# A hybrid attention kernel: batch 0's neighbourhood scores straight from fp32 projections, the others from stacks made behind it

## The chip, the cores and the metric

The kernel runs on one core of one Trainium2 chip. Its time is the device time in microseconds (us) of one execution; the median over the runs counts. The engines are TensorE (PE in the profile; PEld is its weight load, which overlaps its matmuls), VectorE (DVE), ScalarE (ACT), GpSimd (POOL) and SyncE (SP, which here only issues DMAs).

## The reference

Six layers follow each other on an image batch of 4 x 16 x 16 x 64: a full attention, a neighbourhood attention behind a group norm, a self attention, a mixture of experts, a gated attention and a second mixture of experts. The change touches the norm and the second layer:

```python
x = _L0_conv_ref(x, ...)                     # full attention, per batch
x = x + _L1_conv_ref(_gn(x), ...)            # the part that is changed

def _gn(v, G=32, eps=1e-05):                 # norm over image and channel pair
    g = v.reshape(B_, H_, W_, G, C_ // G)
    m = jnp.mean(g, axis=(1, 2, 4), keepdims=True)
    s = jnp.var(g, axis=(1, 2, 4), keepdims=True)
    return ((g - m) / jnp.sqrt(s + eps)).reshape(v.shape)

# neighbourhood attention: 8 heads of 8 features, windows of 7 x 7 pixels
q = proj(wq, bq) / jnp.sqrt(jnp.float32(hd))
scores = jnp.einsum('bnijd,bnijkd->bnijk', q, kn) + bias[None]
probs = jax.nn.softmax(scores, axis=-1)
ctx = jnp.einsum('bnijk,bnijkd->bnijd', probs, vn)
```

## The kernel before, in words

The program writes out every engine's instructions by hand, each engine in its own order, and semaphores tie them together. PE takes its queue strictly in the order written, so a wait holds all that stands behind it.

**Tiling.** A batch has 256 pixels, in two blocks of 128 (`TB` = 2). For one block only 176 pixels (`SPAN`) can lie in a window, so a head's scores are 2 x 176 columns in one PSUM bank; pixels outside the window get a bias of -1e30. There are 32 (batch, head) pairs, numbered n = 8 b + h.

**Two score matrices for each head.** `max_scores` (L589) computes the scores with queries on the partitions, from which DVE takes the negated row maximum `nm1` (`maxima`, L1264). `exact_scores` (L608) computes them again with keys on the partitions, with the maximum added in, so that the exponential can follow without a transpose. The maximum is a value for each query, that is for each column there. POOL therefore writes `diag1`, the identity times `nm1` (L406), and PE multiplies a matrix of ones with it (L628). The bias is added by DVE (`biased`, L1277) for five heads of eight, and by PE, in three bf16 parts (L626), for the heads of `PE_HEADS` = 1, 4, 7. ACT takes the exponential (L1011, L1015), and `attend1` (L645) multiplies four heads at once with the values, each on 32 columns of the array. Maxima run `AHEAD` = 3 heads ahead.

**Stacks.** Scores need fp32 accuracy. Queries and keys are split into three bf16 parts (`high_part` on ACT, L979, and `lower_parts` on DVE, L1228 to L1233), written to DRAM (`store_parts`, L295) and read back in another arrangement (`load_stack`, L306): 9 products of parts, 72 rows, for each head. One bf16 matmul of 72 rows then gives one block's fp32-accurate scores (L602, L622). All four batches go this way. A batch costs 2 stores and 6 loads; those of batch 0 are shared by the SP and ACT queues, the rest are on SP alone, in the order store, store, six loads, batch by batch.

**Norm.** DVE gathers the moments, PE adds up channel pairs (`pair`, L540 and L542), DVE forms the variance, POOL takes the power -1/2 (`group_scale`), ACT and DVE apply it (L974, L1259). Batch 0 is one group, batches 1 to 3 a second. `project` (L555) then gives queries and keys, L585 the values. Between them stand matmuls on ones that compute nothing (`keep_warm`, L450), 2, 4, 6 and 8 of them.

Of the kernel before, what the change touches and what calls it, by code (L numbers as in the profile page):

```python
# [14 lines left out]
P = 128  # L15
B, HW, C = 4, 16, 64
# [9 lines left out]
KS = NT * HD  # L26
VW = 32
MASKED = -1e30

WARM = {"update": 2, "group": 4, "scale": 6, "start": 9, "weights": 2, "stacks": 8, "b_norm": 12, "logits": 2, "loads": 4, "routing": 10,  # L30
# [29 lines left out]
def columns(*pairs):  # L60
    at, where = 0, {}
    for name, width in pairs:
# [6 lines left out]
                     ("first", T * E3), ("slot", 10), ("expert", T * E3), ("fb1", E3 * 2), ("twice", C), ("fb2", PAIRS))  # L69
W0, W0_W = columns(("wvT", C1), ("wo", C), ("wqk1", 2 * C), ("wv1", C))  # L70
WA, WA_W = columns(("w1", E2 * F2), ("wr", E2), ("b2", E2), ("y3", C1), ("gx", 3 * C), ("ga", 3 * C),
                   ("gate", E3))


def hybrid_kernel(nc, x, xt, w8, w0, wa, w3, w2a, w2b, cst, bias_q, bias_k, lnw, out):
    ctx = ExitStack()
    with ctx:
# [14 lines left out]
        qk_parts = nc.dram_tensor("qk_parts", (B, 5, 2 * C, N), BF16, kind="Internal").ap()  # L92
# [11 lines left out]
        half_mem = sb("half_mem", [P, 4992])  # L104
# [13 lines left out]
        def view16(mem, *shape):  # L118
# [5 lines left out]
            if len(shape) == 3:  # L124
# [38 lines left out]
        words = B * NH * N // 2  # L163
        QS, KSt = [stack_mem[0:KS, k * words:(k + 1) * words].bitcast(BF16)
                   .rearrange("r (b h n) -> r b h n", b=B, h=NH) for k in range(2)]
        V1 = view(mid_mem, P, T, NH, VW)
        nm1 = sb("nm1", [P, B, NH, TB], BF16)
        diag1 = view16(half_mem, P, 2, NH, TB * P)
# [100 lines left out]

        def by_dve(n):  # L270

            return n - sum(k % NH in PE_HEADS for k in range(n))
# [10 lines left out]
        QK_BANK = (4, 6, 5, 4)  # L283
# [9 lines left out]
        def store_parts(queue, b, parts, at):  # L293
            queue.wait_ge(sem("qk_part"), 2 * b + parts - 1)
            queue.dma_start(qk_parts[b, at:at + parts].rearrange("i r n -> r i n"), part[:, 0:parts, b * N:b * N + N]) \  # L295
                .then_inc(sem(f"parts_stored{b}"), 16)

        def load_stack(queue, b, pieces):

            queue.wait_ge(sem(f"parts_stored{b}"), 2 * 16)  # L300
            for kind, piece in pieces:
                side, stack = (0, QS) if kind == "queries" else (1, KSt)
                first = 0 if kind == "queries" else piece
                stack = stack[3 * HD * piece:3 * HD * piece + 3 * HD]
                rows = qk_parts[b, first:first + 3].rearrange("i (d s h) n -> s (i d) (h n)", d=HD, s=2)[side]
                queue.dma_start(stack[:, b, :, :].rearrange("r h n -> r (h n)"), rows) \  # L306
                    .then_inc(sem(f"stack_landed{b}"), 16)
# [1419 lines left out]
```

## Time and profile before

| | |
|---|---|
| three runs | 175.31, 176.83, 179.2 us, median 176.83 |
| the profiled execution | 176.17 us, of which the span of the core is 174.4 us |
| TensorE's granted clock, mean | 0.975 of full |
| PE busy | 152.9 us, 88% of the span, 1114 instructions |
| PE weight loads | 106.7 us, 61% |
| DVE busy | 114.5 us, 66%, 382 instructions |
| ACT busy | 71.9 us, 41% |
| POOL busy | 54.2 us, 31%, 82 instructions |

The busy shares are averages over all six layers; the neighbourhood attention takes about 33 to 70 us of the span. Matmuls are pipelined: the duration of one row holds its way through the array, and the cost of one in a dense run is the distance from its start to the next start. An fp32 matmul shows as two records, a bf16 one as one.

### The profile page before, as it was taken

The page shows a single profiled execution, that of the slowest core. Times are in us where ns is not written, and L with a number is a line of the kernel's source. Part 1 is how long each engine was busy: PE and PEld are TensorE (multiplying, and loading weights), DVE is VectorE, ACT ScalarE, POOL GpSimd, SP SyncE. Part 2 cuts the span into 40 slices and gives each one's busy share as a digit, 9 for nine tenths or more (in the row PEclk, how much of TensorE's full clock was granted, in tenths as well). Part 3 has the DMA queues.
Part 4 walks back from the last instruction along what each step waited for, and adds up shares of the span by engine and source line. Part 5 has one row for each costly group of instructions (what it writes and reads, how often), then busy time and mean ns, then how long its engine had stood idle before and what let it go on. Part 6 is the DMA issues. An engine that isn't in the chain of part 4 may idle for free. (4 is left out here: it accounts for less than half of the span.)

```text
span 174.4 us, 3192 instructions
## 1 busy us (share of the span) xinstructions
PE 152.9 (88%) x1114; PEld 106.7 (61%) x1114; DVE 114.5 (66%) x382; ACT 71.9 (41%) x190; POOL 54.2 (31%) x82
## 2 busy tenths in 40 slices
PE   7999879999999997998579999898999876899930
PEld 2698638498888875884235544366794624588720
DVE  2037746688778987637564459648759299886873
ACT  2455404144535354432546243557442600456050
POOL 7052369586556562404300005500002221000030
PEclk9999998799999999999999999999999999999985
DMA  5992052557400000373000000000000000000002
GB/s 162 368 391 49 22 151 55 155 135 194 135 8 6 2 0 4 74 244 124 0 0 0 0 0 0 4 2 0 2 0 0 4 0 0 0 0 0 4 0 62
DMA packets 6954, 10.27 MB, mean 59 GB/s; under 512 B 2703, under 2 KB 5464, under 8 KB 6554
## 3 DMA queue, kind: packets, MB, share of 16 engines
q1 hardware_dynamic: 6736, 9.68, 18.3%
q10 hardware_dynamic: 202, 0.38, 0.9%
q8 instruction: 9, 0.15, 0.4%
q14 instruction: 7, 0.06, 0.1%
HBM read 8.49 MB, written 1.57 MB: 58 GB/s over the span
## 5 line engine op out<-in xcount | busy, mean ns | idle before, releaser
L450 PE MATMUL bank<-onesb 128*128 128x512 bf16 x149 | 38.6, 404 | 1.0 <-DVE onesb L1189 1.0
L450 PEld LDWEIGHTS bank<-onesb 128*128 128x128 bf16 x149 | 14.8, 105 | 16.8 <-issue 3.5
L406 POOL TENSOR_TENSOR half_mem<-identb,nm 128x256 bf16<-128x256 bf16 x32 | 19.5, 614 | 12.4 <-DVE nm L1266 12.2
L1266 DVE TENSOR_REDUCE nm<-bank 128x2 bf16<-128x352 f32 x32 | 16.3, 516 | 5.5 <-PE bank L604 5.2
L1015 ACT ACTIVATE mid_mem<-mid_mem 128x352 f32<-128x352 f32 x20 | 9.9, 497 | 19.1 <-DVE mid_mem L1277 19.1
L622 PE MATMUL bank<-stack_mem 72*128 72x176 bf16 x64 | 13.7, 240 | 0.0
L628 PE MATMUL bank<-half_mem,onesb 128*128 128x176 bf16 x64 | 13.5, 239 | 0.0
L602 PE MATMUL bank<-stack_mem 72*128 72x176 bf16 x64 | 12.7, 241 | 0.3 <-DVE nm L1266 0.3
L604 PE MATMUL bank<-half_mem,identb 128*128 128x176 bf16 x64 | 12.6, 239 | 0.0
L1277 DVE TENSOR_TENSOR mid_mem<-bank,bias_mem 128x352 f32<-128x352 f32 x20 | 10.2, 513 | 0.0
L626 PE MATMUL bank<-bias_mem,identb 128*128 128x176 bf16 x72 | 9.3, 238 | 0.0
L393 POOL TENSOR_TENSOR ln_rsd<-ln_ved,mhalf 128x4 f32<-128x4 f32 x2 | 2.1, 1028 | 21.9 <-DVE ln_ved L1319 21.9
L441 POOL TENSOR_TENSOR mid_mem<-mid_mem,bias_mem 128x256 f32<-128x256 f32 x2 | 1.6, 786 | 23.3 <-DVE mid_mem L1604 23.1
L393 POOL TENSOR_TENSOR ln_rsu<-ln_veu,mhalf 128x4 f32<-128x4 f32 x2 | 2.0, 1012 | 20.6 <-DVE ln_veu L1319 20.6
L1555 DVE TENSOR_SCALAR one_hot<-half_mem,sid 128x1280 fp32r<-128x1280 f32 x8 | 8.2, 1093 | 0.0
L862 PE MATMUL bank<-one_hot,XHL 128*128 128x512 f32 (+1 forms) x24 | 6.1, 381 | 2.1 <-DVE one_hot L1555 2.1
L602 PEld LDWEIGHTS bank<-stack_mem 72*128 72x128 bf16 x64 | 6.2, 98 | 2.6 <-DVE nm L1266 1.5
L645 PE MATMUL bank<-mid_mem 128*32 128x176 f32 x128 | 6.4, 319 | 0.6 <-ACT mid_mem L1011 0.6
L862 PEld LDWEIGHTS bank<-one_hot,XHL 128*128 128x128 f32 x24 | 4.0, 188 | 4.4 <-DVE one_hot L1555 3.9
L622 PEld LDWEIGHTS bank<-stack_mem 72*128 72x128 bf16 x64 | 6.2, 98 | 0.4 <-issue 0.3
L604 PEld LDWEIGHTS bank<-half_mem,identb 128*128 128x128 bf16 x64 | 6.3, 98 | 0.1
L1011 ACT ACTIVATE mid_mem<-bank 128x352 f32<-128x352 f32 x12 | 5.5, 456 | 2.0 <-PE bank L628 2.0
(279 smaller groups left out, 348.5 us busy)
## 6 DMA issues: line engine op xcount, KB each, us to landing
stack_mem<-qk_parts SPq DMA_DIRECT2D x21, 96.0 KB
bias_mem<-bias_q SPq DMA_DIRECT2D x1, 1408.0 KB, 8.1
bias_mem<-bias_k SPq DMA_DIRECT2D x1, 1408.0 KB, 11.1
mid_mem<-w SPq DMA_DIRECT2D x1, 1024.0 KB, 7.2
qk_parts<-half_mem SPq DMA_DIRECT2D x4, 192.0 KB, 2.6
qk_parts<-half_mem SPq DMA_DIRECT2D x4, 128.0 KB, 2.4
mid_mem<-w2b SPq DMA_DIRECT2D x1, 512.0 KB, 8.0
WAs<-wa SPq DMA_DIRECT2D x1, 380.1 KB
```

The costliest lines, as they stand in the source:

```text
L406: pool.tensor_tensor(diag1[:, b % 2, h, :].rearrange("p (q k) -> p q k", q=TB), identb[:, :].unsqueeze(1).to_broadcast([P, TB, P]), nm1[:, ...
L450: pe.matmul(idle[:, :].rearrange("p (k q) -> p k q", k=4), onesb[:, :], onesb[:, :].unsqueeze(1).to_broadcast([P, 4, P]), start=True, stop ...
L602: pe.matmul(dst, QS[:, b, h, q * P:q * P + P], KSt[:, b, h, OFF[q]:OFF[q] + SPAN], start=True, stop=False)
L604: last = pe.matmul(dst, identb[:, :], biasQb[:, h, q * SPAN:q * SPAN + SPAN], start=False, stop=True)
L622: pe.matmul(dst, KSt[:, b, h, k * P:k * P + P], QS[:, b, h, OFF[k]:OFF[k] + SPAN], start=True, stop=False)
L626: pe.matmul(dst, identb[:, :], bias_part[:, i, PE_HEADS.index(h), span], start=False, stop=False)
L628: last = pe.matmul(dst, onesb[:, :], diag1[:, b % 2, h, OFF[k]:OFF[k] + SPAN], start=False, stop=True)
L862: last = pe.matmul(bank[c][:, 0:width], XHL[:, t, :, :].rearrange("p k c -> p (k c)"), G3[:, t % 3, at:at + width], start=(t == 0), stop=( ...
L1015: act.activation(P1[:, n % (2 * QUAD), :], U1[:, n % 3, :], ACT.Exp).then_inc(sem("p1"), 1)
L1266: dve.tensor_reduce(nm1[:, n // NH, n % NH, :], bank[n % 2][:, 0:TB * SPAN].rearrange("p (q k) -> p q k", q=TB), AX.X, ALU.max, negate=Tru ...
L1277: dve.tensor_tensor(U1[:, n % 3, :], bank[2 + n % 2][:, 0:TB * SPAN], biasK[:, n % NH, :], ALU.add) \
L1555: dve.tensor_scalar(G3[:, t % 3, :], iota_f[:, :], sid[:, t:t + 1], None, ALU.is_equal) \
```

## The change

Batch 0 no longer goes through DRAM. Its queries and keys are projected by weights laid out in groups of 32 rows (`by_row_group`), two heads in each group, and kept in fp32 (`Q1` by DVE, `K1` by ACT, with the other head's rows set to zero by `half`). Its scores are fp32 matmuls on 32 rows of the array (`max_direct`, `exact_direct`), those of head n+2's maximum and of head n's exact scores by turns. In batch 0 DVE adds the bias for all eight heads. The norm comes in three groups: batch 0, batch 1, batches 2 and 3. The transposed inputs of the norm lie in banks 0, 5, 6 and 7, and projections of batches 1 to 3 share these banks. Projections, part splits, stores and loads of batches 1 to 3 are written between the heads of batch 0. The third part of the split is made by POOL (`low_part`). For all 32 heads the maximum enters the exact scores by a weight matrix that repeats one column of `nm1` 128 times, multiplied with the identity: four matmuls of 128, 48, 48 and 128 columns, with no work of POOL. The four `keep_warm` runs are gone, and WA's load is ahead of biasK's.

```diff
-WARM = {"update": 2, "group": 4, "scale": 6, "start": 9, "weights": 2, "stacks": 8, "b_norm": 12, ...
+WARM = {"start": 9, "weights": 2, "b_norm": 12, ...
...
+        X1T_BANK = (0, 5, 6, 7)
+        NORM_GROUPS = ((0, 1), (1, 1), (2, 2))
...
@@ gpsimd
+            def low_part(b):
+                c = slice(b * N, b * N + N)
+                pool.wait_ge(sem("qk_mid"), b)
+                pool.tensor_tensor(part[:, 2, c], qkr[:, c], part[:, 1, c], ALU.subtract).then_inc(sem("qk_low"), 1)
...
-                for h in range(NH):
-                    pool.wait_ge(sem("nm1"), b * NH + h + 1)
...
-                    pool.tensor_tensor(
-                        diag1[:, b % 2, h, :].rearrange("p (q k) -> p q k", q=TB),
...
-                    if h == 6 and b >= 2:
-                        rstd("a", b - 2)
-            for b in range(2, B):
                 rstd("a", b)
@@ tensor
+            def exact_biases(n):
+
+                b, h = divmod(n, NH)
+                pe.wait_ge(sem("nm1"), n + 1)
...
+                for k in range(TB):
+                    for q in range(TB):
+                        lo, hi = max(OFF[k], q * P), min(OFF[k] + SPAN, q * P + P)
+                        pe.matmul(bank[2 + n % 2][:, k * SPAN + lo - OFF[k]:k * SPAN + hi - OFF[k]],
+                                  nm1[:, b, h, q:q + 1].to_broadcast([P, P]), identb[:, lo - q * P:hi - q * P],
+                                  start=(k == 0 and q == 0), stop=False, skip_group_check=True)
...
+            def direct_scores(n):
+
+                if n + 2 < NH:
+                    max_bias(n + 2)
+                if n + 2 == QUAD:
+                    pe.wait_ge(sem("k1"), 2)
+                exact_biases(n)
+                for i in range(TB):
+                    if n + 2 < NH:
+                        mx = max_direct(n + 2, i)
+                    ex = exact_direct(n, i)
...
+            first_two()
+            pair(1)
+            attend0(3)
+            turn_x1(2)
             for n in range(B * NH + LAG):
-                b, h = divmod(n, NH)
-                if b < B:
+                if n < NH:
+                    direct_scores(n)
+                elif n < B * NH:
                     if n + AHEAD < B * NH:
-                        max_scores((n + AHEAD) // NH, (n + AHEAD) % NH)
-                    exact_scores(b, h)
+                        max_stacked(n + AHEAD)
+                    exact_stacked(n)
+                if n == 0:
+                    turn_x1(3)
+                    project(1)
+                if n == 1:
+                    pair(2)
+                if n == 3:
+                    project(2)
+                if n == 5:
+                    project(3)
+                if n == 6:
+                    max_stacked(8)
+                if n == 7:
+                    max_stacked(9)
+                    pe.wait_ge(sem("qk_rest"), B - 1)
+                    values1(TB, T, bank[7])
+                    max_stacked(10)
```

How the order moves, first on PE behind batch 0's norm. Before, from its projection on (`XN1` is the normed input, `X1` the output of the first layer, `gn_e` the norm's moments; L450 computes nothing):

```order
L555 MATMUL bank<-XN,W0s 128x256
L473 MATMUL bank<-Cs,S_P 128x128 x4
L531 MATMUL bank<-Cs,X 64x128 x4
L524 MATMUL bank<-VX,S_PT 128x65 x4
L450 MATMUL bank<-onesb 128x512 x2
L531 MATMUL bank<-Cs,X 64x128 x2
L450 MATMUL bank<-onesb 128x512 x4
L540 MATMUL bank<-gn_e,Cs 64x6
L542 MATMUL bank<-gn_e,Cs 64x3
L450 MATMUL bank<-onesb 128x512 x6
L555 MATMUL bank<-XN,W0s 128x256 x3
L585 MATMUL bank<-W0s,XN 128x64 x8
```

In the changed kernel, from the same projection on (L596 is the bias of a maximum, L603 the fp32 scores of a maximum, L562 values):

```order
L548 MATMUL bank6<-XN1,WAs 128x256
L550 MATMUL bank4<-XN1,WAs 128x256
L471 MATMUL bank7<-Cs,S_P 128x128 x4
L529 MATMUL bank5<-Cs,X1 64x128 x2
L562 MATMUL bank2<-WAs,XN1 128x64 x2
L596 MATMUL bank0<-half_mem,identb 128x176 x2
L596 MATMUL bank1<-half_mem,identb 128x176 x2
L603 MATMUL bank0<-stack_mem 128x176
L603 MATMUL bank1<-stack_mem 128x176
```

The first two heads' maxima now stand right behind batch 0's projection, ahead of the last product of the first layer, the norm of the other batches and their values. Next, PE where batch 0 hands over to batch 1 in the changed kernel (L625 is the repeated column, L639 exact fp32 scores, L676 a stacked maximum, L703 `attend1`):

```order
L625 MATMUL bank2<-identb,nm1 128x128
L639 MATMUL bank2<-stack_mem 128x176 x2
L596 MATMUL bank0<-half_mem,identb 128x176 x2
L676 MATMUL bank0<-stack_mem 128x176 x2
L703 MATMUL bank4<-mid_mem 32x176 x8
L625 MATMUL bank3<-identb,nm1 128x128
L625 MATMUL bank3<-identb,nm1 128x48 x2
L625 MATMUL bank3<-identb,nm1 128x128
L639 MATMUL bank3<-stack_mem 128x176 x2
```

The first row that needs batch 1's stacks (L676) stands behind the exact scores of head 6, and all of PE behind it waits for them. On the SP queue, the stores and loads before:

```order
L322 DMA bias_mem<-bias_q 128x2816
L323 DMA bias_mem<-bias_k 128x2816
L324 DMA WAs<-wa 65x1497
L295 DMA qk_parts<-half_mem 128x2x256
L295 DMA qk_parts<-half_mem 128x3x256
L306 DMA stack_mem<-qk_parts 24x2048 x3
L295 DMA qk_parts<-half_mem 128x2x256
```

and in the changed kernel:

```order
L326 DMA bias_mem<-bias_q 128x2816
L327 DMA WAs<-wa 65x1945
L328 DMA bias_mem<-bias_k 128x2816
L300 DMA qk_parts<-half_mem 128x2x256
L300 DMA qk_parts<-half_mem 128x3x256
L310 DMA stack_mem<-qk_parts 24x2048 x6
L300 DMA qk_parts<-half_mem 128x2x256
```

Batch 0's two stores and its loads (three here, three on the ACT queue) are gone; the first stores are now those of batch 1.

## Rows read from the trace of the kernel before

**Rows 1.** Stretches: us, busy time of each engine (x), PE clock, DMA share, GB/s.
```profile
30.00:35.00 5.00, 4.69 (x28) 2.52 (x28) 3.29 (x9) 0.60 (x1) 2.94 (x8) 0.75 0.53 148
50.00:60.00 10.00, 9.96 (x138) 8.80 (x136) 8.51 (x26) 4.64 (x11) 6.09 (x10) 1.00 0.01 3
```

**Rows 2.** Timeline of PE: start us, us, engine, line, operation, out<-in.
```profile
17.95 0.65 PE L555 MATMUL bank<-XN,W0s 65*128 65x256 f32 x2
19.06 0.60 PE L531 MATMUL bank<-Cs,X 128*64 128x128 f32 x4
...
23.63 0.28 PE L540 MATMUL bank<-gn_e,Cs 65*64 65x6 f32 x2 [0.37 <-DVE gn_e L1256]
...
26.54 1.56 PE L555 MATMUL bank<-XN,W0s 65*128 65x256 f32 x6 [1.02 <-ACT XN L974]
27.94 2.43 PE L585 MATMUL bank<-W0s,XN 65*128 65x64 f32 x16
30.16 3.07 PE L450 MATMUL bank<-onesb 128*128 128x512 bf16 x8
33.06 0.24 PE L602 MATMUL bank<-stack_mem 72*128 72x176 bf16 x1
33.14 0.24 PE L604 MATMUL bank<-half_mem,identb 128*128 128x176 bf16 x1
```

**Rows 3.** Timeline of PE, steady heads of the neighbourhood attention.
```profile
40.11 0.80 PE L645 MATMUL bank<-mid_mem 128*32 128x176 f32 x16
40.85 0.25 PE L602 MATMUL bank<-stack_mem 72*128 72x176 bf16 x1
...
42.25 0.24 PE L622 MATMUL bank<-stack_mem 72*128 72x176 bf16 x1
...
67.47 0.24 PE L628 MATMUL bank<-half_mem,onesb 128*128 128x176 bf16 x1
```

**Rows 4.** Half-microsecond stretches, columns as in the first group.
```profile
27.00:27.50 0.50, 0.50 (x4) 0.43 (x3) 0.00 (x0) 0.23 (x1) 0.50 (x1) 1.00 0.38 90
...
37.00:37.50 0.50, 0.50 (x9) 0.50 (x7) 0.50 (x2) 0.01 (x1) 0.23 (x2) 1.00 0.29 86
...
48.00:48.50 0.50, 0.50 (x8) 0.49 (x7) 0.28 (x1) 0.18 (x1) 0.50 (x1) 1.00 0.07 8
```

**Rows 5.** Timeline of the SP queue: stores and loads of the query and key pieces.
```profile
29.39 0.89 SPq L295 DMA_DIRECT2D qk_parts<-half_mem  x2
31.98 2.34 SPq L306 DMA_DIRECT2D stack_mem<-qk_parts  x6
...
44.13 2.35 SPq L306 DMA_DIRECT2D stack_mem<-qk_parts  x6
```

**Rows 6.** Timeline of ACT.
```profile
18.64 0.38 ACT L979 ACTIVATE half_mem<-bank 128x256 bf16<-128x256 f32 x1
...
25.92 1.01 ACT L974 ACTIVATE XN<-bank,gn_nb,gn_r 64x256 f32<-64x256 f32 x2 [6.06 <-POOL gn_nb L361]
```

**Rows 7.** The chain that ended last, one piece: start us, us, what.
```profile
124.10 0.33 PE bank L820 x2
```

**Rows 8.** Timeline of PE: fp32 matmuls of 8 columns, then short bf16 ones.
```profile
138.09 1.40 PE L841 MATMUL bank<-WAs,XFb 65*128 65x8 f32 x12
139.35 1.24 PE L450 MATMUL bank<-onesb 128*128 128x512 bf16 x5
140.85 0.20 PE L849 MATMUL bank<-ohb,prefixb 128*128 128x64 bf16 x1 [0.26 <-DVE ohb L1533]
140.88 0.32 PE L851 MATMUL bank<-ohb,onesb 128*128 128x56 bf16 x7
141.07 1.24 PE L450 MATMUL bank<-onesb 128*128 128x512 bf16 x5
```

**Rows 9.** Timeline of POOL.
```profile
21.10 2.19 POOL L370 TENSOR_TENSOR bias_mem<-bias_mem 128x1056 f32<-128x1056 f32 x1 [2.90 <-DVE half_mem L1233]
```

**Rows 10.** Timeline of DVE.
```profile
65.10 0.75 DVE L1335 TENSOR_SCALAR XNa<-X,ln_mva,ln_rsa 128x64 f32<-128x64 f32 x2 [0.60 <-POOL ln_rsa L393]
```

More of the change, by code:

```diff
@@ L26 @@
 KS = NT * HD
+GROUP = 32
 VW = 32
 MASKED = -1e30
-WARM = {"update": 2, "group": 4, "scale": 6, "start": 9, "weights": 2, "stacks": 8, "b_norm": 12, "logits": 2, "loads": 4, "routing": 10,
+WARM = {"start": 9, "weights": 2, "b_norm": 12, "logits": 2, "loads": 4, "routing": 10,
         "selection": 11, "c_norm": 34, "c_steps": {1: 1, 2: 3, 3: 3}, "a_steps": {3: 4},
@@ L268, in hybrid_kernel, with on_pe @@
         table = sb("table", [1, 1])
+        def on_pe(n):
+            return n >= NH and n % NH in PE_HEADS
         def by_dve(n):
-            return n - sum(k % NH in PE_HEADS for k in range(n))
+            return n - sum(on_pe(k) for k in range(n))
         def normed(engine, s, b):
@@ L293, in store_parts, with load_stack @@
         def store_parts(queue, b, parts, at):
[L294 to L298, printed above, removed]
+            queue.wait_ge(sem("qk_mid" if parts == 2 else "qk_low"), b)
+            queue.dma_start(qk_parts[b - 1, at:at + parts].rearrange("i r n -> r i n"),
+                            part[:, 0:parts, b * N:b * N + N]).then_inc(sem(f"parts_stored{b}"), 16)
+        def load_stack(queue, b):
             queue.wait_ge(sem(f"parts_stored{b}"), 2 * 16)
[L301 to L307, printed above, removed]
+            for piece in range(3):
+                for side, stack in ((0, QS), (1, KSt)):
+                    first = side * piece
+                    rows = qk_parts[b - 1, first:first + 3].rearrange("i (d s h) n -> s (i d) (h n)", d=HD, s=2)[side]
+                    queue.dma_start(stack[3 * HD * piece:3 * HD * piece + 3 * HD, b - 1, :, :]
+                                    .rearrange("r h n -> r (h n)"), rows).then_inc(sem(f"stack_landed{b}"), 16)
         def final(sp):
@@ L566, in _ @@
             scores0(3)
-            pair(0, 0, 1)
+            pair(0)
             turn_p0(2)
@@ new lines, in max_stacked @@
+            def max_stacked(n):
+                b, h = divmod(n, NH)
+                if h == 0:
+                    pe.wait_ge(sem(f"stack_landed{b}"), 6 * 16)
+                max_bias(n)
+                for q in range(TB):
+                    last = pe.matmul(bank[n % 2][:, q * SPAN:q * SPAN + SPAN], QS[:, b - 1, h, q * P:q * P + P],
+                                     KSt[:, b - 1, h, OFF[q]:OFF[q] + SPAN], start=False, stop=(q == TB - 1),
+                                     skip_group_check=True)
+                last.then_inc(sem("mx1"), 1)
@@ L630, in exact_scores, with exact_stacked @@
+            def exact_stacked(n):
+                b, h = divmod(n, NH)
+                exact_biases(n)
+                for k in range(TB):
+                    last = pe.matmul(bank[2 + n % 2][:, k * SPAN:k * SPAN + SPAN], KSt[:, b - 1, h, k * P:k * P + P],
+                                     QS[:, b - 1, h, OFF[k]:OFF[k] + SPAN], start=False, stop=(k == TB - 1),
+                                     skip_group_check=True)
                 last.then_inc(sem("s1"), 1)
```

345 lines of the change are left out of this document (193 added, 152 removed).

## The prediction

> **What bounds the kernel now.** I read the stretches first. In the steady part of the neighbourhood attention PE is busy 9.96 of 10 us, DVE 8.51, ACT 4.64, POOL 6.09 [rows 1]: PE bounds it, and DVE is close behind. The timeline of PE gives the pace. From batch 1's first exact scores at 42.25 to the last head's at 67.71, 24 heads take 25.4 us, 1.06 each [rows 3]. The start is another matter. Batch 0 is projected at 17.95, but its first score matmul starts at 33.06; right ahead of it PE does eight matmuls that compute nothing, from 30.16 on [rows 2], at a mean clock of 0.75 of full [rows 1], while the last traffic of batch 0's loads had ended by 27.5 [rows 4]. So 15 us lie between projection and scores: first the way through DRAM, then the norm, projection and values of the other batches and the padding. The change aims at this hole, and all else is a side effect. Everything behind 70 us is the same work and moves along with the end of this stage.
>
> I price the change at one mark, the start of head 8's exact scores, 42.25 before [rows 3], and then the pace behind it.
>
> **What one matmul costs.** Four prices.
> - A bf16 matmul of 176 columns: 0.08, start to start (33.06 to 33.14) [rows 2].
> - Short bf16 matmuls with weights of their own: eight, from 140.85 to 141.07, so 0.028 each [rows 8]. The repeated column takes four of 128, 48, 48 and 128 columns in place of two of 176: 2 x 0.057 + 2 x 0.028 = 0.17 against 0.16. That holds if a weight matrix that reads one column 128 times loads like an ordinary one. No row shows such a load. Ends: 0.028 for a load, and 0.105, the pitch of fp32 records whose 8 columns cannot hide their loads (12 from 138.09 to 139.35) [rows 8]. I take the lower, since type and size are those of the bf16 rows. Ending at the upper, four loads cost 0.42.
> - One fp32 matmul of 176 columns on 32 rows, called P. Alone, by the 192-column one at 0.33 [rows 7]: 0.30. If two on different row groups overlap, their loads of 128 fp32 columns remain, two records of 0.105: 0.21. The lowest end is `attend1`, eight such matmuls on four column groups from 40.11 to 40.85, 0.09 each [rows 3]; but its weights have 32 columns. I take 0.25, between the two near ones. Two rounds of 0.30 leave 0.14 of those 0.74 us for going into the tiled array and out again; I charge that per head.
> - Small fp32 work: 0.105 a record [rows 8], 0.44 for a projection of 256 columns (0.33 x 256 / 192).
>
> Here rows and a rule of the skill part. Every bf16 load in the trace is hidden or comes at 0.028 us. The Trainium skill (TensorE: Matmul & The Clock Gate, LDWEIGHTS) gives a load by its columns, 128 / 1.2 GHz = 107 ns, whatever its rows; the fp32 rows agree (105 ns), the bf16 rows don't. The same page (Weight-path perf modes) grants the fast load to 128 non-fp32 weights at any column step from -1,023 to 1,024, which includes a step of zero; no row here shows that step. By the first rule the sum ends 6 us later, by the second as forecast.
>
> **Batch 0 on PE.** After the projection at 17.95 stand `turn_p0(3)` and `turn_x1`, of which the first half is done at about 19.3 [rows 2]; a second projection (0.44) and two value matmuls (0.42) put the first maxima at 20.2. K1 needs two ACT passes of 0.38 after the exponential, which are done by about 19.4, as ACT was free at 18.64 [rows 6]: no wait. Then:
> - `first_two`: 4 x 0.08 + 4P + 0.14 = 1.45.
> - six heads with both matrices: 2 x 0.08 + 0.17 + 4P + 0.14 = 1.47, together 8.8.
> - two heads with exact scores alone, both matmuls on one row group, so 2 x 0.30: 0.91 each, 1.8.
> - between them: `pair` twice 0.84, `attend0(3)` 8 records 0.84, `turn_x1` twice 0.5, three projections 1.3, `attend1` 0.74, the other values 12 records 1.26, four stacked maxima 1.25. Sum 6.7.
>
> Total 18.8, so head 8 at 39.0 if PE never waits. I add 0.6 for in-order waits on DVE and ACT, which now carry eight bias additions, the norm and the splits between the heads: 39.6, **2.65 us earlier**. Ends: P = 0.30 adds 28 x 0.05 = 1.4, so 41.0; the other end is set by the stacks.
>
> **Batch 1's stacks.** `pair(1)` starts at 21.65. Before, that step stood at 23.63 [rows 2] and the normed input at 25.92 [rows 6], 2.3 later: 24.0. `project(1)` stands on PE behind `attend0(3)`, two turns and head 0: 22.1 + 0.84 + 0.5 + 1.47 = 24.9. From projection to first store it took 26.54 [rows 2] to 29.39 [rows 5], 2.85: 27.75. To the loads 2.6 (29.39 to 31.98), and from the loads to the end of their traffic 4.0 (44.13 to 48.1) up to 5.4, when the next batch's store runs among them (31.98 to 37.4) [rows 4, 5]. They land at 34.4 to 35.8. Before, PE was at its keep-warms when such a load came; now PE stops at head 8's maximum. It gets there at 20.2 + 18.8 - 0.31 - 0.74 - 0.91 - 3 x 0.31 - 1.26 = 34.9, and those terms, 4.2 us, stand behind it. The stacks therefore allow 38.6 to 40.0, and my 39.6 lies inside. The third part's subtraction goes to POOL: 2.19 us for 1056 columns [rows 9] makes 0.53 for 256, which is inside the 2.85. SP no longer carries batch 0; batches 2 and 3 have 8 heads, over 8 us, for the same chain, and stay hidden.
>
> **Behind the mark.** 24 heads x 0.013 = +0.3. POOL's 32 products vanish. PE did not wait for them while it was at 9.96 of 10, but `rstd` stood in their queue and DVE waited 0.60 for it [rows 10], in two batches; I take -0.3 (ends 0 and -1.2). Removing the keep-warms is inside the mark. WA's load is now ahead of biasK's. Zero: the first layer hides it, which runs until the projection at 17.95 [rows 2]; a WA later than that would delay everything by as much as it is late.
>
> **Sum.** 176.17 (profiled execution, span 174.4) - 2.65 + 0.3 - 0.3 = 173.5. The median of the runs is 176.83, 0.66 above that execution, so 174.2 by it. I say **173.8**. About 2% is what a measurement of this kernel can tell from no change, that is 173.3 and 180.4 around the median.
>
> **Rivals.**
> - *A, the forecast*, 172.8 to 174.8: chance 0.45.
> - *B, the repeated column loads slowly.* Place: `exact_biases`, all heads. At 0.105 a load a head costs 0.26 more: 24 x 0.26 = 6.3 behind the mark, 8 x 0.26 = 2.1 in batch 0, part of it in the wait for the stacks. That is 173.8 + 7 to 8, about **181**, slower. It decides from about 0.07 us a load on, where 24 x 0.11 eats the gain. For it: PE has no slack (9.96 of 10) and nothing shows such a load. Against: all bf16 loads here are fast. Chance 0.15.
> - *C, batch 0 runs at its dear end*: the row groups don't overlap (head 8 at 41.0, +1.4), or the clock halves between 20 and 36 us, as it did in 30 to 35 [rows 1], where PE had waited 1.02 us at 26.54 [rows 2] before it; 3.5 us at half clock cost 1.7. About **175.5**. For it: the padding is gone and the heads hang on DVE. Against: PE has useful work almost without a hole. Chance 0.23.
> - *D, the overlap is good and POOL's relief is whole*: head 8 at 38.7 and -1.0 behind it, about **172.0**. Chance 0.12.
> - *E, in-order stalls in batch 0 of 3 us more than I priced*, DVE being the bound there: 177. Chance 0.05.
>
> Range 171.5 to 178.5: it leaves out B, and little else. Faster by over 2%: D, a fair part of A, and what noise adds, 0.38. Slower by over 2%: B mostly, 0.14. Within: 0.48.
>
> **What would show it.** First score matmul at about 20.2, not 33; head 0 to 7 at about 1.5 us each; fp32 score records of two lines that overlap; a wait on DMA of under 1 us ahead of the first stacked maximum; head 8's exact scores at about 39.6; four short matmuls of 0.17 us a head and a pace of 1.06 to 1.08 behind it; clock 1.00 from 20 to 40 us. Wrong would make it: short matmuls over 0.07 us apart (B), heads of batch 0 at 1.8 us or a clock of 0.5 (C), stacks that land after 37.

## The result and the profile after

The change made the kernel **slower**: 183.28 us median (181.89, 182.44, 184.12 and 190.90), against 178.01 for the kernel before in the same comparison; the ratio is 1.038 [1.019, 1.057]. The ratios in this document leave out executions over 1.5% above the fastest of their kernel in the same comparison (here 190.90, and 179.2 and 188.3 of the kernel before); by the medians it is 1.030. The prediction, 173.8 with a range up to 178.5, was wrong. The profiled execution took 182.44 us, its span is 180.6 (before 174.4), its mean granted clock 0.919 (before 0.975).

The profile page of the changed kernel gives PE's busy share and its clock in 40 slices of 4.5 us each, in tenths:

```profile
PE   7999998999999998899598999899999897899920
...
PEclk9999999555599999999969999999999969999985
```

Slices 8 to 11, which hold the second half of batch 0's heads and the first of batch 1's, are at half clock, while PE counts as fully busy. The stretches show it more finely (us, busy time of PE, PEld, DVE, ACT, POOL, then clock, DMA share, GB/s):

```profile
20.00:25.00 5.00, 4.70 (x47) 3.83 (x45) 4.27 (x15) 0.99 (x3) 2.85 (x4) 1.00 0.00 0
...
30.00:35.00 5.00, 5.00 (x36) 3.67 (x36) 2.67 (x7) 2.03 (x6) 2.00 (x2) 0.67 0.68 185
35.00:40.00 5.00, 5.00 (x34) 3.38 (x32) 1.77 (x4) 1.01 (x3) 0.67 (x1) 0.50 0.43 113
40.00:45.00 5.00, 5.00 (x30) 4.62 (x30) 1.60 (x4) 0.99 (x2) 0.00 (x0) 0.50 0.52 154
...
50.00:55.00 5.00, 4.96 (x76) 4.28 (x74) 3.98 (x10) 2.34 (x5) 0.00 (x0) 1.00 0.00 0
```

At 0.50 the clock is 1.2 GHz, at 1.00 it is 2.4. By the half-microsecond stretches it is low from 31.7 to 48.8, **17.07 us without a break**; before it was low for 3.41 us there, from 29.1 to 32.5, mostly under the keep-warms [rows 1]. The timeline of PE, over the same piece:

```profile
19.80 0.47 PE L596 MATMUL bank<-half_mem,identb 128*128 128x176 bf16 x4
...
26.65 0.33 PE L596 MATMUL bank<-half_mem,identb 128*128 128x176 bf16 x2
26.81 0.33 PE L625 MATMUL bank<-identb,nm 128*128 128x128 bf16 x4
27.07 0.41 PE L603 MATMUL bank<-stack_mem 32*128 32x176 f32 x1
27.07 0.41 PE L639 MATMUL bank<-stack_mem 32*128 32x176 f32 x1
...
27.86 0.33 PE L596 MATMUL bank<-half_mem,identb 128*128 128x176 bf16 x2
...
29.84 0.70 PE L557 MATMUL bank<-XN,WAs 65*128 65x256 f32 x2 [0.69 <-ACT XN L1050]
...
39.01 1.54 PE L639 MATMUL bank<-stack_mem 32*128 32x176 f32 x4
...
44.73 0.50 PE L625 MATMUL bank<-identb,nm 128*128 128x128 bf16 x4
...
54.25 0.33 PE L625 MATMUL bank<-identb,nm 128*128 128x128 bf16 x4
54.41 0.62 PE L632 MATMUL bank<-bias_mem,identb 128*128 128x176 bf16 x6
...
73.32 0.41 PE L761 MATMUL bank<-Cs,XNa 128*64 128x128 f32 x2
```

The first scores start at 19.80, with their bias (before 33.06 [rows 2]), and a head with both matrices takes 27.86 - 26.65 = 1.21 us. Then PE waits 0.69 us for batch 2's normed input, and from 31.7 on everything takes nearly twice as long. Batch 0's last scores on 32 rows end at 39.01 + 1.54 = 40.55, and the clock is back only at 48.8, so 8.2 of the 17.07 us lie behind them, under values and stacked heads. Head 8's exact scores, the mark of the prediction, start at 44.73: 2.5 us later than before, not 2.65 earlier. The next stage (L761, the former L682, which stood at 69.00) starts at 73.32.

### The profile page after: what moved, and what is told of

It reads as the page before. It is cut to its first block and busy times, and to the rows that moved or that the text cites. A ratio compares the mean times of both kernels' runs of the same rounds, so it can differ in the third digit from the quotient of the medians.

```text
span 180.6 us, 3277 instructions
## 1 busy us (share of the span) xinstructions
PE 161.4 (89%) x1178; PEld 113.6 (63%) x1178; DVE 114.1 (63%) x384; ACT 73.0 (40%) x193; POOL 37.4 (21%) x55
## 3 DMA queue, kind: packets, MB, share of 16 engines
q1 hardware_dynamic: 5956, 9.18, 17.4%
## 5 line engine op out<-in xcount | busy, mean ns | idle before, releaser
L448 PE MATMUL bank<-onesb 128*128 128x512 bf16 x129 | 35.0, 420 | 1.0 <-DVE onesb L1285 1.0
L448 PEld LDWEIGHTS bank<-onesb 128*128 128x128 bf16 x129 | 13.0, 107 | 15.6 <-issue 4.1
L1371 DVE TENSOR_TENSOR mid_mem<-bank,bias_mem 128x352 f32<-128x352 f32 x23 | 11.9, 517 | 3.9 <-PE bank L639 3.1
L625 PE MATMUL bank<-identb,nm 128*128 128x128 bf16 (+1 forms) x128 | 11.5, 212 | 0.0
L596 PE MATMUL bank<-half_mem,identb 128*128 128x176 bf16 x64 | 11.1, 262 | 0.0
L403 POOL TENSOR_TENSOR ln_rsa<-ln_vea,mhalf 128x2 f32<-128x2 f32 x4 | 2.8, 705 | 37.5 <-DVE ln_vea L1413 37.5
L625 PEld LDWEIGHTS bank<-identb,nm 128*128 128x128 bf16 x128 | 9.0, 104 | 1.2 <-issue 1.1
L639 PE MATMUL bank<-stack_mem 32*128 32x176 f32 x32 | 8.9, 409 | 0.0
L676 PE MATMUL bank<-stack_mem 72*128 72x176 bf16 x48 | 8.7, 267 | 0.0
L686 PE MATMUL bank<-stack_mem 72*128 72x176 bf16 x48 | 8.1, 253 | 0.0
L703 PE MATMUL bank<-mid_mem 128*32 128x176 f32 x128 | 7.1, 342 | 0.6 <-ACT mid_mem L1107 0.6
L596 PEld LDWEIGHTS bank<-half_mem,identb 128*128 128x128 bf16 x64 | 5.7, 107 | 2.9 <-issue 2.6
L603 PE MATMUL bank<-stack_mem 32*128 32x176 f32 x32 | 6.7, 358 | 0.0
L639 PEld LDWEIGHTS bank<-stack_mem 32*128 32x128 f32 x32 | 6.2, 235 | 0.3
```

The lines of the kernel that those rows point to most:

```text
L448: pe.matmul(idle[:, :].rearrange("p (k q) -> p k q", k=4), onesb[:, :], onesb[:, :].unsqueeze(1).to_broadcast([P, 4, P]), start=True, stop ...
L596: pe.matmul(bank[n % 2][:, q * SPAN:q * SPAN + SPAN], identb[:, :], biasQb[:, n % NH, q * SPAN:q * SPAN + SPAN], start=(q == 0), stop=Fals ...
L625: pe.matmul(bank[2 + n % 2][:, k * SPAN + lo - OFF[k]:k * SPAN + hi - OFF[k]], nm1[:, b, h, q:q + 1].to_broadcast([P, P]), identb[:, lo - ...
L639: return pe.matmul(bank[2 + h % 2][:, k * SPAN:k * SPAN + SPAN], K1[r, h // QUAD, k * P:k * P + P], Q1[r, OFF[k]:OFF[k] + SPAN], start=Fal ...
L676: last = pe.matmul(bank[n % 2][:, q * SPAN:q * SPAN + SPAN], QS[:, b - 1, h, q * P:q * P + P], KSt[:, b - 1, h, OFF[q]:OFF[q] + SPAN], sta ...
L686: last = pe.matmul(bank[2 + n % 2][:, k * SPAN:k * SPAN + SPAN], KSt[:, b - 1, h, k * P:k * P + P], QS[:, b - 1, h, OFF[k]:OFF[k] + SPAN], ...
```

## The experiments

Two theories stood after this. **K, the kind of work**: batch 0's fp32 scores, which work on 32 rows of the array ("thin" below; "full-height" is work on all 128), don't keep the clock up as the keep-warms and full-height matmuls did. **S, the stall**: the 0.69 us wait lets the clock fall, whatever kind of work is about it. Rival to both: the repeated column or the missing POOL products cost time. All differences below are against the kernel named at the top of each diff; a ratio is against the kernel before. In the table, "low" is the time at half clock up to 95 us in the profiled execution, in us, and "next stage" the start of the stage behind the neighbourhood attention, in us.

| kernel | median us | ratio | low | next stage |
|---|---|---|---|---|
| before | 178.0 | 1 | 3.4 | 69.00 |
| changed | 183.28 | 1.038 [1.019, 1.057] | 20.5 | 73.32 |
| fill1 | 177.1 | 0.999 [0.991, 1.006] | 3.4 | 66.37 |
| fill3 | 178.79 | 1.017 [1.006, 1.028] | 0 | 70.36 |
| nostall | 181.81 | 1.034 [1.025, 1.044] | 13.7 | 71.40 |
| waitfill | 181.8 | 0.993 [0.989, 0.997], six of twelve | 34.1 (one of the other six) | not compared |
| column_only | 177.42 | 1.002 [0.996, 1.008] | 3.4 | 69.49 |
| full_rows | 175.89 | 0.989 [0.985, 0.994] | 0 | 67.34 |
| no_padding | 179.98 | 1.018 [1.009, 1.028] | 20.5 | 72.42 |

The medians are over all executions and come from several chips, so the ratios compare the kernels. The other parts of the change (three norm groups, the third part on POOL, the order of WA's load) were not run alone; fill1 has all of them and reaches the next stage 2.63 us earlier than before.

### One or three matmuls that compute nothing behind each head of batch 0

```diff
--- the changed kernel
                 if n < NH:
                     direct_scores(n)
+                    if n >= 5:
+                        pe.wait_ge(sem("qk_rest"), 1)
+                    keep_warm(1, bank[4] if n < 5 else bank[5])
```

> The changed kernel with one bf16 matmul of 512 columns on ones, which computes nothing, behind each of batch 0's eight heads (0.21 us each at full clock, 1.7 in all). Theory K (the kind of work): batch 0's fp32 matmuls on 32 rows are what the chip does not count as enough work, so the clock falls to half and stays there until the bf16 heads come. It expects the half-clock time of 17.1 us (31.5 to 48.6) to shrink in part or wholly, and the kernel at 175 to 181 us. Theory S (the stall): the clock falls because PE stood still for 0.69 us ahead of batch 2's projection. The stall is still there (the filler covers 0.2 us of it), so S expects 15 us or more at half clock and 182 to 184 us. Theory P (PE is simply full, the clock only shifts): slower than the changed kernel by the 1.7 us added.

> The same with three such matmuls behind each head: 5.2 us more PE work at full clock, of which 0.6 us fills the stall ahead of batch 2's projection. Theory K: dense bf16 work of 0.64 us in each 1.8 us keeps the clock at full, no half-clock stretch between 20 and 50 us; head 8's exact scores at about 38.3 + 4.6 = 43, the kernel 178 to 180. Theory S: the stall is filled too, so it expects the same; this run alone does not part them, the one with the projection moved does. If neither holds, the half-clock stretch stays near 17 us and the kernel is at 187 or more.

fill3 has `keep_warm(3, ...)`. With one for each head, the page's clock row is

```profile
PEclk9999999999999999999699999999999999999995
```

and PE's timeline where the changed kernel was at half clock:

```profile
34.80 0.33 PE L596 MATMUL bank<-half_mem,identb 128*128 128x176 bf16 x2
34.96 0.32 PE L676 MATMUL bank<-stack_mem 72*128 72x176 bf16 x2
35.21 0.81 PE L703 MATMUL bank<-mid_mem 128*32 128x176 f32 x16
...
39.47 0.33 PE L625 MATMUL bank<-identb,nm 128*128 128x128 bf16 x4
39.63 0.32 PE L686 MATMUL bank<-stack_mem 72*128 72x176 bf16 x2
...
66.37 0.41 PE L764 MATMUL bank<-Cs,XNa 128*64 128x128 f32 x2
```

The half clock in the attention is gone, with eight matmuls of 0.23 us added. So is the wait of 0.69 us, since PE comes to batch 2's projection with its input ready, and theory S, which forecast 182 to 184 us with that wait in place, was not put to the test. The next stage starts 69.00 - 66.37 = 2.63 us earlier than before; the prediction's own figure for it was 2.65. Much of that is lost again behind it: the clock halves for 3.41 us at 83.5 to 87, where it did not before, and the span ends at 173.1, only 1.3 below 174.4. And three of its ten executions took 189 to 192 us at a mean clock of 0.88 to 0.89, outside the ratio; the filler does not prevent these. Three matmuls for each head delay the next stage by 4.0 us more, 66.37 to 70.36, of which 16 x 0.23 = 3.7 are the matmuls themselves; in the attention there was no more clock to win.

### The stall taken away

```diff
--- the changed kernel
-                if n == 3:
+                if n == 4:
                     project(2)
...
-                if n == 3:
+                if n == 4:
                     lower_parts(2)
...
-                    if n == 4:
+                    if n == 5:
                         high_part(2)
```

> The changed kernel with batch 2's projection one head later on PE (behind head 4 and not head 3), its split one head later on ACT and DVE. That takes the 0.69 us stall at 29.1 away and adds no work. Theory S: the clock does not fall at 31.5, the 17 us at half clock go, worth up to 8.5 us, and the kernel comes to 174 to 177. Theory K: the clock falls all the same, within some microseconds of 31.5, stays at half until the bf16 heads run, and the kernel stays at 181 to 184.

Batch 2's projection stands one head later, when its input is ready. The 0.69 us wait is gone, and the clock now stays at 1.00 past 31.7. But PE, at full pace, reaches batch 1's stacks before they have landed:

```profile
35.47 0.33 PE L596 MATMUL bank<-half_mem,identb 128*128 128x176 bf16 x2 [1.89 <-DMA stack_mem<-qk_parts]
...
37.24 1.54 PE L639 MATMUL bank<-stack_mem 32*128 32x176 f32 x4
```

```profile
35.00:40.00 5.00, 4.53 (x36) 3.34 (x37) 2.25 (x5) 0.99 (x2) 0.67 (x1) 0.63 0.50 125
40.00:45.00 5.00, 5.00 (x36) 5.00 (x36) 2.14 (x5) 0.99 (x2) 0.00 (x0) 0.50 0.54 151
45.00:50.00 5.00, 5.00 (x68) 4.34 (x66) 2.63 (x6) 1.94 (x5) 0.00 (x0) 0.84 0.18 43
```

The first fence is from the timeline of PE, the second the stretches behind it. Behind this wait the clock is half from 36.3 to 46.6, 10.24 us. So the fall moved with the stall, which speaks for S as to when it falls. How long it stays low is not told by a stall of 1.9 us, nor here by thin work alone: the only thin scores left, those of the row at 37.24, end at 38.78, and 7.8 of the 10.24 us lie behind them.

### The stall of the stacks covered

```diff
--- nostall
                 if n == 6:
+                    pe.wait_ge(sem("qk_rest"), 1)
+                    keep_warm(8, bank[5])
                     max_stacked(8)
```

> The changed kernel with batch 2's projection one head later, as in the run before, and with eight bf16 matmuls that compute nothing (1.7 us at full clock) ahead of the wait for batch 1's stacks, which was 1.89 us with the projection moved. The fp32 heads of batch 0 stay as they are, with no filler between them. Theory S (a stall makes the clock fall, thin work then keeps it down): no stall over 0.4 us is left between 20 and 50 us, so the clock stays at full there, head 8's exact scores come at 39 to 40, and the kernel takes 174 to 176. Theory K (the kind of work alone makes it fall): the clock falls between 30 and 40 us all the same, as nothing was put between the heads, and the kernel takes 180 or more.

Six of its twelve executions took 175.70 to 176.64 us at a mean clock of 0.962 to 0.972, and the ratio of 0.993 [0.989, 0.997] is theirs alone. The six others took 187 to 192 us at a clock of 0.88 to 0.90, as did one of the changed kernel's four (190.90 at 0.877) and three of fill1's ten; the median of all twelve is 181.8. The profiled execution is one of the six dear ones, and shows where it loses its time:

```profile
17.00:17.50 0.50, 0.50 (x6) 0.50 (x5) 0.39 (x1) 0.45 (x1) 0.44 (x1) 0.90 0.06 23
51.00:51.50 0.50, 0.50 (x10) 0.26 (x12) 0.24 (x1) 0.00 (x0) 0.00 (x0) 0.50 0.88 233
51.50:52.00 0.50, 0.50 (x16) 0.24 (x8) 0.28 (x1) 0.00 (x0) 0.00 (x0) 0.97 0.57 170
```

The clock fell at 17.4, ahead of the whole neighbourhood attention, and stayed low until 51.5, 34.1 us. That is the picture of the changed kernel, entered earlier: the clock is down ahead of batch 0's scores and stays down through them. It comes back 4.5 us after the eight full-height matmuls begin, at 47.04. The six good ones fit S, which forecast 174 to 176 us, by their time and mean clock; no trace shows their clock from 20 to 50 us.

### The repeated column alone

```diff
--- the kernel before
-                for h in range(NH):
-                    pool.wait_ge(sem("nm1"), b * NH + h + 1)
...
-                pe.wait_ge(sem("diag1"), n + 1)
+                pe.wait_ge(sem("nm1"), n + 1)
...
+                    for q in range(TB):
+                        lo, hi = max(OFF[k], q * P), min(OFF[k] + SPAN, q * P + P)
+                        pe.matmul(bank[2 + n % 2][:, k * SPAN + lo - OFF[k]:k * SPAN + hi - OFF[k]],
+                                  nm1[:, b, h, q:q + 1].to_broadcast([P, P]), identb[:, lo - q * P:hi - q * P],
...
-                    last = pe.matmul(dst, onesb[:, :], diag1[:, b % 2, h, OFF[k]:OFF[k] + SPAN],
```

> The kernel before with one part of the change alone: the maximum enters by the repeated column, four short matmuls, and POOL's 32 products go. The forecast's step: +0.013 us a head on PE, -0.3 us from POOL, so within 0.5 us of the kernel before, clock as there (3.4 us at half). Rival B of the prediction would have it 7 to 8 us slower; the trace of the changed kernel already shows four of them in 0.25 us, so that is not expected.

1.002 [0.996, 1.008], with POOL's 32 products gone: no cost and no gain. The row at 54.25 of the changed kernel shows the price directly. Four matmuls with a repeated column take 54.41 - 54.25 = 0.16 us at full clock, 0.04 each with weights of their own. Rival B of the prediction is refuted. The 0.3 us that I gave to POOL's relief is too little for this ratio to show. In the profile the wait of 0.60 us [rows 10] is gone, yet the next stage starts no earlier (69.49, before 69.00).

### Batch 0's scores on all 128 rows

```diff
--- the changed kernel
-        K1 = view(stack_mem, P, NH // QUAD, N)
+        K1 = view(stack_mem, P, NH, N)
...
-                return pe.matmul(bank[h % 2][:, q * SPAN:q * SPAN + SPAN], Q1[r, q * P:q * P + P],
-                                 K1[r, h // QUAD, OFF[q]:OFF[q] + SPAN], start=False, stop=(q == TB - 1),
+                return pe.matmul(bank[h % 2][:, q * SPAN:q * SPAN + SPAN], Q1[:, q * P:q * P + P],
+                                 K1[:, h, OFF[q]:OFF[q] + SPAN], start=False, stop=(q == TB - 1),
...
-                for s in range(NH // QUAD):
+                for s in range(first, end):
                     act.activation(K1[:, s, :], bank[6][:, 0:N], ACT.Copy,
-                                   scale=Cs[:, CST["half"]][:, s:s + 1]).then_inc(sem("k1"), 1)
+                                   scale=Cs[:, CST["head"]][:, s:s + 1]).then_inc(sem("k1"), 1)
```

> The changed kernel with batch 0's fp32 scores on all 128 rows of the array (K1 in eight versions, each with all rows but its head's set to zero) in place of 32-row groups: the same products, but no two at once. Each head goes from 0.66 to about 1.2 us of fp32 matmuls, so batch 0 costs some 4 us more at full clock, of which about 2 lie in the wait for the stacks that is there at full clock. Theory K, that few rows of the array are what counts: the clock does not stay at half for 17 us, and the kernel takes 177 to 180, less than the changed one although it does more. If the clock stays down as in the changed kernel, the rows do not matter and it takes 186 or more.

Same result, same order of work; ACT writes eight copies of the keys, each with the rows of all other heads set to zero, and every score matmul spans all 128 rows. Two matmuls cannot overlap now, and each costs 0.30 (L602 and L637 are the maximum's and the exact scores):

```profile
28.13 0.33 PE L596 MATMUL bank<-half_mem,identb 128*128 128x176 bf16 x2
28.29 0.33 PE L624 MATMUL bank<-identb,nm 128*128 128x128 bf16 x4
28.45 0.52 PE L602 MATMUL bank<-stack_mem 128*128 128x176 f32 x2
28.80 0.46 PE L637 MATMUL bank<-stack_mem 128*128 128x176 f32 x2
29.10 0.46 PE L602 MATMUL bank<-stack_mem 128*128 128x176 f32 x2
29.40 0.46 PE L637 MATMUL bank<-stack_mem 128*128 128x176 f32 x2
29.70 0.32 PE L596 MATMUL bank<-half_mem,identb 128*128 128x176 bf16 x2
...
67.34 0.41 PE L758 MATMUL bank<-Cs,XNa 128*64 128x128 f32 x2
```

```profile
PEclk9999999999999999999999999999999999999975
```

A head costs 29.70 - 28.13 = 1.57 us in place of 1.21, and yet the kernel has the lowest ratio of those here: the first fence is its timeline, the second its page's clock row, with no half clock anywhere until the end. From 20 to 60 us PE waits nowhere for 0.25 us or more, since it reaches batch 2's input and the stacks later. All ten of its executions lie between 175.1 and 177.2, on the chip on which waitfill had six of twelve at 187 and more. The forecast for theory K, 177 to 180, was above that.

### The padding taken out of the kernel before

```diff
--- the kernel before
-            keep_warm(WARM["update"], bank[7])
...
-            keep_warm(WARM["group"], bank[7])
...
-            keep_warm(WARM["scale"], bank[7])
...
-                    keep_warm(WARM["stacks"], bank[0])
+                    pass
```

> The kernel before without the 20 bf16 matmuls on ones that the change took out (2, 4, 6 and 8, between batch 0's norm and the first scores). The forecast took them for a cost of the path. Simple theory: PE reaches the first scores up to 2.9 us earlier (30.16 in place of 33.06) and the kernel is 1 to 3 us faster. Clock theory: the stalls of 0.5 to 2 us between 22 and 27 us are open then, the clock falls there, and since the heads of this kernel are dense bf16 it comes back within 3.4 to 7 us; the saving and the loss about cancel, 176 to 179 us.

```profile
27.54 2.93 PE L555 MATMUL bank<-XN,W0s 65*128 65x256 f32 x6 [2.42 <-ACT XN L971]
...
33.56 0.35 PE L599 MATMUL bank<-stack_mem 72*128 72x176 bf16 x1
```

Without the 20 matmuls that compute nothing, the first scores start 0.5 us *later* (33.56, before 33.06 [rows 2]), since projection and values run at half clock behind waits of 0.96, 1.23 and 2.42 us. The clock is low from 24.0 to 41.1, again 17.07 us, and 7.5 us of that lie behind the start of the ordinary, stacked heads. So thin fp32 work is not the only work that leaves it low. Whether it falls there for PE's idle time or for the missing full-height work is not told apart.

### Thin and full fp32 matmuls in the kernel before

```diff
--- the kernel before
+            def probe(count, rows=32):
+                flat1 = X1[:, :, :].rearrange("p t c -> p (t c)")
+                for i in range(count):
+                    r = slice(32 * (i % 2), 32 * (i % 2) + 32) if rows == 32 else slice(0, P)
+                    pe.matmul(bank[i % 2][:, 0:SPAN], flat1[r, 0:P], flat1[r, P:P + SPAN], start=True, stop=True)
...
-                    keep_warm(WARM["stacks"], bank[0])
+                    probe(30)
+                    probe(30, P)
```

This is probe_switch. probe32 has 60 matmuls on 32 rows there, and 100 in place of the keep-warms of a later norm; probe128 has 30 and 55 on 128 rows.

> The kernel before with its eight keep-warms ahead of the first scores replaced by 60 fp32 matmuls of 176 columns on 32 rows, on two row groups by turns, and its 34 ahead of the gated attention by 100 of them (16.5 us at full clock). Their results are not used. Only the clock counts, the time is longer by design. In the kernel before the clock is at half when the first place is reached and back at full 3.4 us later. Theory K: in the first place the clock stays at half for all of the 20 us; in the second it falls within some microseconds. Theory S: no stall in either, so it comes back in the first as before, and does not fall in the second.

> The same with 30 and 55 fp32 matmuls of 176 columns on all 128 rows (0.30 us each at full clock). Theory K: the clock comes back in the first place within about 4 us and does not fall in the second. Theory S: the same here; only the run on 32 rows parts the two. If the clock stays down here too, it is fp32 as such and not the number of rows.

> The kernel before with its eight keep-warms ahead of the first scores replaced by 30 fp32 matmuls of 176 columns on 32 rows (two row groups by turns) and right behind them 30 on all 128 rows, results not used. The clock is at half when this place is reached, as it was in the probe on 32 rows, where it stayed at half for all of 18 us. Theory K2 (work on few rows does not make the clock fall, but it cannot bring it back either; work on all rows can): half clock through the first 30 (9 us), full within about 4 us of the first matmul on 128 rows. If fp32 as such cannot bring it back, it stays at half through both and returns with the bf16 heads. If the clock is at full on entry, the run tells nothing.

Each probe was run once. probe32 (201.22 us), PE's timeline, and the stretches about it:

```profile
30.24 17.97 PE L457 MATMUL bank<-X 32*128 32x176 f32 x120
...
121.49 15.19 PE L457 MATMUL bank<-X 32*128 32x176 f32 x200
```

```profile
35.00:40.00 5.00, 5.00 (x37) 5.00 (x36) 0.00 (x0) 0.00 (x0) 0.00 (x0) 0.50 0.48 117
...
130.00:135.00 5.00, 5.00 (x70) 5.00 (x68) 0.98 (x4) 0.13 (x1) 0.32 (x1) 1.00 0.02 5
```

In the first place the clock fell at 30.2, just as the thin work began, and it stayed at half for all of it and 5.9 us beyond, 23.9 us in all; that it would come back as before, which S had forecast, did not happen. In the second the clock was full when it began, and it stayed full for 15.19 us of nothing but thin work. K as I had put it, that thin work lets the clock fall, is refuted by this row. probe128 (190.94 us) had no half clock at all up to 95 us, so it says that full-height fp32 work kept the clock, and nothing on how it comes back. probe_switch (193.75 us) does both in one place; the thin ones run to about 39, the full ones behind them:

```profile
29.50:30.00 0.50, 0.50 (x4) 0.50 (x3) 0.50 (x2) 0.00 (x0) 0.46 (x1) 0.50 0.00 0
...
38.00:38.50 0.50, 0.50 (x6) 0.50 (x6) 0.00 (x0) 0.00 (x0) 0.00 (x0) 0.50 0.00 0
...
42.00:42.50 0.50, 0.50 (x4) 0.50 (x3) 0.00 (x0) 0.00 (x0) 0.00 (x0) 0.50 1.03 242
...
43.00:43.50 0.50, 0.50 (x5) 0.50 (x5) 0.00 (x0) 0.00 (x0) 0.00 (x0) 0.99 0.85 249
```

The clock was half from 29.4 on, before the thin matmuls began at 30.21, half through 9 us of them, and back at 43.0, 4 us after the full-height ones took over, with the type and the columns unchanged; at 43.0 probe32, still at thin work, was at half. What differs is the rows of the array and, with them, that two thin matmuls overlap and two full-height ones do not; these two are not told apart, and each probe is one execution.

### More padding in a later norm

```diff
--- full_rows, and the kernel before
-    "b_norm": 12
+    "b_norm": 17
```

> The best version so far: batch 0's scores in fp32 on all 128 rows, and 17 in place of 12 bf16 matmuls that compute nothing ahead of the second feed-forward's features, where PE stands still for 1.26 us; five take 1.07 of it. Theory: the 3.4 us dips of the clock that most runs show behind that stall cost up to 1.7 us each, and the filler lies in idle time. It expects a clock of 0.975 to 0.985 in nearly all runs, 174 to 175.5 us, a ratio of 0.98 to 0.985 to the kernel before. If the dips there have another cause, it is where the run on all rows was, at 0.989.

> The kernel before with the same 17 in place of 12 and nothing else, as a control. The runs of the kernel before fall into three clusters, near 175.3, 177.0 and 178.8 us, with clocks of 0.975, 0.965 and 0.948, one dip of 3.4 us apart. If the stall is a cause of these dips, the dearer clusters thin out and the ratio is 0.985 to 0.995; if not, it is 1.00.

The aim was the clock's later dips. full_rows with it: 175.41 us median of 12, ratio 0.993 [0.989, 0.998], against full_rows' 0.989 [0.985, 0.994]. The kernel before with it: 177.22, 1.002 [0.996, 1.007]. No gain can be told in either. The order of the first two ratios means little: the one of full_rows counts executions of the kernel before up to 179.06 us, the other, on another chip, only up to 177.22, and by the medians it is the other way round, 175.41 / 177.22 = 0.990 and 175.89 / 177.18 = 0.993. The profiled execution of full_rows with 17 has a dip of 3.4 us at 144.5 that full_rows' has not.

## Why the prediction was wrong

**What held.** The prices of PE were right or a little dear. The first score work came at 19.80 (forecast 20.2). A head with both matrices took 1.21 (forecast 1.47), since two fp32 matmuls on different row groups do overlap: four and the way out of the tiled array cost 27.86 - 27.07 = 0.79, and 0.10 more lies ahead of them (27.07 - 26.81 = 0.26 for a repeated column of 0.16), together 0.89 where I had 4 x 0.25 + 0.14 = 1.14. The repeated column cost 0.16 (0.17). Stores and loads went out at 26.87 and 29.69 (27.75 and 30.35) and in nostall, where PE waits for them, had landed at 35.47 (34.4 to 35.8). With the clock kept, in fill1, the mark stands at 39.47 (39.6), with a pace behind it near before's: 66.37 - 39.47 = 26.90, against 69.00 - 42.25 = 26.75. That the mark fits so well is partly luck: six heads at 0.26 less save 1.6 us, and the eight added matmuls ahead of the mark, which were not in the forecast, cost 8 x 0.23 = 1.8.

For weights at a step of zero I had set two rules of the Trainium skill (TensorE: Matmul & The Clock Gate) against each other: Weight-path perf modes, by which they get the fast load, and LDWEIGHTS, 107 ns by their 128 columns. The 0.04 us from one such matmul to the next sides with the fast load. The record of one such load lasts 104 ns on average in the profile's page, so 107 ns fits how long a load takes here, and not what it costs among others. The Trainium skill (same page, Part 3: Packing small matmuls) measured 3.07 times for four row groups at once; the trace agrees that groups overlap, with 4 x 0.30 / 0.79 = 1.5 times for two with the way out of the tiled array included, and 0.30 / 0.15 = 2 times in probe32's dense run.

**The step that failed** is the clock: the sum has no term for it, and the term of rival C was far too small. C said that "the clock halves between 20 and 36 us" and "3.5 us at half clock cost 1.7". The sum took up the padding with "Removing the keep-warms is inside the mark", that is as a pure gain. C's argument against was "PE has useful work almost without a hole"; PE was busy 5.00 of 5 us from 35 to 45 us and the clock was half all the same. The mechanism was named; its size was wrong by five times (17.07 us in place of 3.5), because I took how long the clock stays low from the kernel before, where eight full-height matmuls that compute nothing stood in that very place and the stacked heads behind them. Even for that kernel it was low: in the execution profiled with `b_norm` at 17, the same stretch of that kernel was low for 6.83 us. In the changed kernel it was 17.07. The sum of what it did, against the forecast of 173.5 for the profiled execution, which took 182.44:

- up to the mark, 44.73 - 39.6 = 5.1 us. 13.0 of the 17.07 us at half clock lie there and are worth up to 6.5 (half of their time); the cheaper heads give some of it back.
- from the mark to the next stage, 73.32 - 44.73 = 28.6, forecast 26.75 + 0.3 = 27.1: 1.5 us, put down to the last 4.1 us at half clock, which are worth up to 2.0.
- behind it, 180.6 - 73.32 = 107.3, and before 105.4: 1.9 us, and the 0.3 us that the forecast took off for POOL. There are two new dips of 3.4 us, at 89.5 and at 144; such dips come in executions of the kernel before too, so that this one had none there is in part luck.

Together 8.8 of the 8.9 us.

**What the runs show of the cause.** The loss has two parts. First the clock falls: in the changed kernel 1.9 us behind the end of a wait of 0.69, in nostall 0.9 us behind one of 1.89. Then it stays down through batch 0's 32-row fp32 work, as it does in probe32 and in the first half of probe_switch. The return takes time of its own behind that work: 4 us of dense full-height matmuls in probe_switch, 5.9 of stacked heads in probe32, and 7.8 and 8.2 us of values and stacked heads in nostall and the changed kernel. Taking away only the first trigger found a second (nostall). One full-height matmul a head (fill1) or full-height scores (full_rows) left no half clock in the attention in the profiled executions; fill1 still had three dear executions of ten, full_rows none of ten. That the padding pays in its old place is shown apart from the change: without it the kernel before is 1.8% slower, nearly half of the change's 3.8%.

**What stays open.** It is open why some waits are followed by a fall and others are not: the one of 1.02 us at 26.54 [rows 2] was, in the kernel before, and probe128, which has the same work up to that place, kept its clock; and whether fill1 and full_rows work by what they put on the array or by the stalls that they fill up is not separated, as they do both. Why the return takes 4 us in one run and 8 in another is open too, and so is what makes the clock fall ahead of the attention in the dear executions of the changed kernel, fill1 and waitfill. What sets the later dips (83 to 93, 144 to 150), which come with nearly every kernel in some execution and still came with five more matmuls, was not found.

## The better version

full_rows beats both kernels: 0.989 [0.985, 0.994] of the one before (0.993 by the medians), a gain that is clear of noise but small, and some 4 to 5% under the change as it was. It keeps the change's structure and gives up the row groups, the part that looked cheapest by the matmul's price: 0.36 us a head more, about 2 us in all, and in its profile none of the 17 us at half clock.

## What to carry to other kernels

Matmuls that compute nothing are part of a clock budget: when a change deletes them, price the stretch at both clocks, or put something full-height in their place. Packing small matmuls into row groups saves array time (1.21 us a head against 1.57) but once the clock has fallen, thin work held it at half for as long as it lasted in every run here; where it replaces full-height work, price this as a rival of its own size, by the length of the thin stretch and the 4 to 8 us that the return took behind it, not by the dip that the old trace shows. And when a stage speeds up, list the waits that it newly runs into (here ACT's norm, then the stacks): each is a place where the clock may fall.

## What was not expected of the hardware

- The clock stayed at half for 17.07 us on end (23.9 in probe32) with PE busy 5.00 of 5 us by the records. 15.19 us of thin work that began at full clock stayed at full.
- fp32 matmuls of 176 columns cost 0.30 us on 128 rows, and on 32 rows 15.19 / 100 = 0.15 each when two row groups alternate, at full clock.
- A stationary operand that reads one column 128 times cost no more than an ordinary one: four such matmuls, of 352 columns together, took 0.16 us, as much as two of 176 columns at 0.08 [rows 2].
- A half-clock stretch of 3.4 us costs the kernel before about 1.7 us. This is an estimate from its executions, which gather at 175.3, 177.0 and 178.8 us, at mean clocks of 0.975, 0.965 and 0.947; one dip more lowers the mean by 3.4 x 0.5 / 175 = 0.01.
